# Query and key parts kept beside each other per row in DRAM: a 3 KB store per row, loads of one part of eight rows in 1 KB packets

## The reference, cut to what matters

```python
x = x + xattn0(layernorm(x), ctx, ctx)         # 16 heads of 8, softmax over 128 keys
x = x + ffn0(layernorm(x))                     # one of 8 experts per token
x = x + xattn1(layernorm(x), ctx, ctx)         # the same with a causal mask
x = x + ffn1(layernorm(x))                     # two of 8 experts per token, SiLU gate
# inside an attention: score = einsum('bhqd,bhkd->bhqk', q, k) / sqrt(8)
```

## Time and profile before

| | |
|---|---|
| time, median of 3 runs | 794.02 us (790.98 to 795.57) |
| the profiled execution | 793.19 us, its span 791.5 us |
| TensorE busy | 619.9 us (78%) |
| VectorE, ScalarE, GpSimd busy | 483.2, 392.2, 359.4 us |
| DMA | 65087 packets, 87.58 MB |
| stages in the span | projection to about 113 us, attention 0 to 261, one-expert stage to 380, attention 1 to 607, two-expert stage to 771, the end to 791 |

### The profile page before, as it was taken

One profiled execution on the slowest core, in us unless ns is written; L12 is line 12 of the kernel. 1 busy time (PEld: TensorE's weight loads), 2 busy tenths in 40 slices (PEclk: granted clock), 3 DMA queues, 4 the chain that ended last, 5 costly groups with the idle time before them and its releaser, 6 DMA issues.

```text
span 791.5 us, 22885 instructions
## 1 busy us (share of the span) xinstructions
PE 619.9 (78%) x8205; PEld 473.8 (60%) x8205; DVE 483.2 (61%) x1255; ACT 392.2 (50%) x901; POOL 359.4 (45%) x555
## 2 busy tenths in 40 slices
PE   1583548999999599999899888888740999999970
PEld 1352236777776354554566666666530999999970
DVE  1462257777773367667667988889534455555535
ACT  0684335777777224443367666666630444444430
POOL 5384351111010234445245577877874455555650
PEclk9697677999999699999799999999955999999995
DMA  3479850434400593577711543400011222222219
GB/s 75 123 249 177 189 193 3 109 95 111 96 4 2 108 268 143 188 277 247 295 49 40 102 106 106 103 26 26 26 44 54 55 66 70 59 63 67 63 34 318
DMA packets 65087, 87.58 MB, mean 111 GB/s; under 512 B 11209, under 2 KB 52433, under 8 KB 64977
## 3 DMA queue, kind: packets, MB, share of 16 engines
q1 hardware_dynamic: 56400, 75.04, 33.9%
q0 software_dynamic: 4352, 8.99, 3.6%
q10 hardware_dynamic: 4224, 2.10, 0.9%
HBM read 43.99 MB, written 41.96 MB: 109 GB/s over the span
## 4 chain that ended last, share of the span: by engine, by line
PE 36%; DVE 13%; issue 6%; POOL 5%; ACT 5%; DMA 2%; SPq 1%; ACTq 0%; POOLq 0%; DVEq 0%
PE bank L1567 12%; PE bank L1575 6%; PE bank L1410 5%; DVE nm L929 3%; POOL sorted_in L1130 2%; ACT pr L814 2%; POOL pr L1100 1%; DMA kk<-results 1%; DVE e0ch L1351 1%; PE bank L697 1%; PE bank L1555 1%; PE bank L753 1%; PE bank L1391 1%; PE bank L726 1%; PE bank L715 1%
## 5 line engine op out<-in xcount | busy, mean ns | idle before, releaser
L814 ACT ACTIVATE pr<-bank 128x512 f32<-128x512 f32 x256 | 146.9, 603 | 76.0 <-PE bank L700 73.4
L929 DVE TENSOR_REDUCE nm<-bank 128x8 f32<-128x1024 f32 x128 | 155.7, 1221 | 38.9 <-PE bank L674 37.7
L1567 PE MATMUL bank<-exxt,qq 128*128 128x128 f32 (+1 forms) x864 | 109.2, 277 | 0.7 <-ACT exxt L1605 0.7
L1567 PEld LDWEIGHTS bank<-exxt,qq 128*128 128x128 f32 (+1 forms) x864 | 101.3, 185 | 1.1 <-ACT exxt L1605 1.1
L1100 POOL TENSOR_SCALAR_AFFINE_SELECT pr<-pr 128x1024 f32<-128x1024 f32 x64 | 69.7, 1090 | 56.8 <-ACT pr L814 56.1
L1541 POOL DMA_INDIRECT results<-exy,exre x72 | 71.3, 990 | 29.8 <-issue 29.0
L715 PE MATMUL bank<-pr,values 128*9 128x128 f32 x2048 | 81.6, 278 | 2.4 <-POOL pr L1100 2.4
L697 PE MATMUL bank<-qq,kk 48*128 48x128 bf16 x1024 | 75.4, 221 | 3.4 <-ACT pr L814 2.4
L1410 PE MATMUL bank<-e0ch,expert_w 128*128 128x512 f32 x128 | 70.8, 635 | 6.4 <-DVE e0ch L1351 6.4
L700 PE MATMUL bank<-mt,pick 64*128 64x128 bf16 x1024 | 75.5, 221 | 0.0
L1642 DVE TENSOR_TENSOR exhi<-bank,exsi 128x384 f32<-128x384 f32 x72 | 40.1, 557 | 54.7 <-PE bank L1567 43.6
(11 more groups left out here) (209 smaller groups left out, 1160.9 us busy)
## 6 DMA issues: line engine op xcount, KB each, us to landing
sorted_in<-values SPq DMA_DIRECT2D x25, 715.0 KB, 5.7
k_parts<-pj_parts SPq DMA_DIRECT2D x16, 384.0 KB, 4.3
kk<-k_parts SPq DMA_DIRECT2D x64, 96.0 KB
qq<-q_parts SPq DMA_DIRECT2D x64, 96.0 KB
exx<-sorted_in SPq DMA_DIRECT2D x72, 65.0 KB
kk<-k_parts SPq DMA_DIRECT2D x64, 64.0 KB
qq<-q_parts SPq DMA_DIRECT2D x64, 64.0 KB
q_parts<-pj_parts SPq DMA_DIRECT2D x8, 384.0 KB, 4.1
```

The costliest lines, as they stand in the source:

```text
L814: act.activation(probs[c], st_bank[(n * NC + c) % ST][:], ACT.Exp, scale=scale).then_inc(exp_s, 1)
L929: dve.tensor_reduce(neg_max[n % 2][:, u * 2 * C4:(u + 1) * 2 * C4], score_banks(n, u).rearrange("q (h k) -> q h k", k=T), AX_X, ALU.max, n ...
L1567: mm = pe.matmul(to[q.p][0:fn, f * T:(f + 1) * T], own_w[q.p][:, w0 + f0:w0 + f0 + fn], x, start=True, stop=True)
```

## The change

The DRAM tensors get the part as the last index but one, so that the three parts of one row (of one head) lie beside each other, 3 KB in one piece. The store becomes one piece of 3 KB per row. One part of a head's row is now followed by the other two, so a load can take only one part of eight rows with the eight heads of a half, and each row is read in eight pieces of 1 KB that lie 3 KB apart, into 8 KB in one piece in the tile. A part that three slots need is a load for each slot, as before; the number of loads stays 12 per side.

```diff
-QK_IN = 16 * 2 * 2 * 2 * len(RUNS)
+QK_IN = 16 * 2 * 2 * 6

-        q_parts = scratch("q_parts", (NG, 3, DH, H, GT), BF16)
-        k_parts = scratch("k_parts", (2, NG, 3, DH, H, GT), BF16)
+        q_parts = scratch("q_parts", (NG, DH, H, 3, GT), BF16)
+        k_parts = scratch("k_parts", (2, NG, DH, H, 3, GT), BF16)

             for slot, part, count in runs:
-                by_half = src[part:part + count].rearrange("c d (a i) t -> a (c d) i t", a=2)
-                for s in range(2):
-                    row = s * HALF + slot * DH
-                    for u in range(2):
-                        heads = slice(u * C4, (u + 1) * C4)
-                        eng.dma_start(tile[g % QK_BUFS][row:row + count * DH, heads], by_half[s][:, heads]).then_inc(signal, 16)
+                for c in range(count):
+                    by_half = src[:, :, part + c, :].rearrange("d (a i) t -> a d i t", a=2)
+                    for half in range(2):
+                        row = half * HALF + (slot + c) * DH
+                        eng.dma_start(tile[g % QK_BUFS][row:row + DH], by_half[half]).then_inc(signal, 16)

-            eng.dma_start(to.rearrange("c d h t -> (d h) c t"), tile[:]).then_inc(signal, 16)
+            eng.dma_start(to.rearrange("d h c t -> (d h) (c t)"), tile[:].rearrange("p c t -> p (c t)")).then_inc(signal, 16)
```

## The result

The changed kernel takes 814.12 us (median of 4 runs, 808.23 to 817.54) where the kernel before takes 793.87 beside it (790.98 to 795.57): 1.0256 times the time before, 95% interval 1.0208 to 1.0304. It is slower by some 20 us. Its profiled execution took 817.03 us with a span of 815.3, against 793.19 and 791.5 before, so the two spans differ by 23.8 us, 3.6 more than the medians do.

What follows compares the result with a forecast made beforehand. The projection's second half was taken as bound by transfers, attention 0 by TensorE. Profiled 793.2 us, plus 16 for the projection and 7.5 for attention 0, gave 816.7, say 817 us; eight in ten: 794 to 866.

Steps and rivals of the forecast that it cites:

- the likeliest case: Whole kernel: a group's 24 loads take 17 to 24.6 us, total 804 to 866 us; chance 0.50.
- Eight engines a load, and the issue time not the limit: Part loads: each runs over 8 engines, 192 completions a group instead of 288; SP's 9.6 us of issue stays the faster.
- T = 19.0: Part loads, both stages: a group's 24 loads take 19.0 us instead of 12.7, bounded by 8.8 and 30.7.
- the queued row at equal crowding: Part loads: same bytes at the queued packet cost of before, 48 x 0.39 = 18.7 us a group.
- (a): Part loads: crowding becomes complete, a group takes 25 to 31 us; about 917 us at 28.9; chance 0.12.
- (b): Part loads: nothing seen, a group takes up to 13.5 us, SP's issue stays the pace; 793 +- 4; chance 0.14.
- (d): Part loads: in between, 14 to 17 us a group; projection +4 to +11, attention 0 nothing; 797 to 804; chance 0.14.
- Projection, +17 for loads and -1 for stores: Projection: three bound turns each lose 5.7 us to slower loads, less 1 for cheaper stores, +16 us.
- The gain of 0.4 us a turn: Projection stores: 3 KB packets take 2.9 instead of 3.3 us a turn, 1.2 us over three turns.
- Attention 0, +7.5 us as waits for tiles at the first scores of groups 4 to 7: Attention 0: five groups of 19.0 us loads outrun 16.7 us compute periods; group 7 arrives at 234.6, needed at 227.1.
- One-expert stage and attention 1, 0 to 3 us: Later stages: key loads grow from 15.2 to some 28 us but are covered; cost 0, at most 3 us.
- Rival (c): Projection: fewer store packets end SP's full-queue hold-ups, 5.8 us, plus 1.2 of cheaper stores; 786 us; chance 0.10.

Runs made afterwards that it cites:

- the fourth experiment: Kernel before, with loads of one eight-row part (8 KB a row) only for groups 0 to 2 in the projection; 810.43 us, 1.0218.
- the second experiment: Kernel before with only the store changed, to 3 KB pieces, its loads kept (attention values wrong, timing valid); 791.34 us, 0.9996.
- the third experiment: Kernel before, layout and store kept, every load taking one part of eight rows, 8 KB in one piece per row; 818.57 us, 1.0324.
- 5.: Kernel before, with loads of one eight-row part only for groups 3 to 7 in attention 0; 805.01 us, 1.0129.
- 6.: Kernel before, with only the key loads of groups 3 to 7 in attention 0 taking one eight-row part; 802.48 us, 1.0118.
- experiment 11: Kernel before, with all eight heads of a half in one load, six loads a side instead of 12; 802.46 us, 1.0127.
- experiment 12: Kernel before, its loads reordered so that neighbours in the queue write different halves of the rows; 786.28 us, 0.9917.
- 7.: Changed kernel, with the late loads of both attentions issued in four lots of six per group; 811.49 us, 1.0254 to the kernel before.

## Why the prediction was right, and where only by luck

817.0 us was forecast, in 804 to 866 for the likeliest case and 794 to 866 in all; 814.12 was measured. Step by step:

- **Eight engines a load, and the issue time not the limit**: right. The completions fell by 4 a load.
- **T = 19.0**: 17.7 measured in attention 0 (17.2 from first packet to last), and 0.10 us a packet, the value at which the forecast said that the sum would hold. In the projection it is not one value: 19.7, 15.8 and 14.3 us where before it is 13.1, 14.4 and 13.5. The bounds were 8.8 and 30.7, so taking the queued row at equal crowding (48 x 0.39) was the good choice. (By the port rule of the Trainium skill, page SBUF — State Buffer, section "Door 1: The DMA port swizzle", T would have been 28.9 us, an estimate load by load; the trace disagrees with it. That loads in flight on different rows overlap is my reading.) Rivals (a) and (b) fall with it, and (d), whose T of 14 to 17 is near that of the projection, falls by the time: 797 to 804 was its range.
- **Projection, +17 for loads and -1 for stores**: +11.35 measured. By the sum's own form T = 17.7 gives 3 x 5.0 x 0.9 - 1 = +12.5. But the two terms were each too small: narrow loads alone cost 20.3 us there (the fourth experiment, with 8 KB pieces), and 9 us of it come back with the layout of the change (20.3 - 11.35; single profiles, whose start of attention 0 scatters by 4 us). The gain of 0.4 us a turn counted the stores' packets; what a store also does is to hold SP when the queues are full. Freeing that was worth nothing behind the loads of before (the second experiment). That it is what gives back the 9 us behind narrow loads fits the 23.9 and 8.6 us of the third experiment, but isn't shown: the 1 KB pieces of the loads changed with it.
- **Attention 0, +7.5 us as waits for tiles at the first scores of groups 4 to 7**: this step failed. By its own form T = 17.7 leaves 1 us. 11.3 was measured, and not one wait of TensorE for `kk` or `qq`: group 3's first scores come at 171.68, on time for a stage that starts 11.35 us later. In its place stand stalls of the instruction stream, 8.0 us, with the half clock behind them, 3.3. That narrow loads in this stage bring them on is shown (5., 6.: some 10 us each, with the gaps; the fourth experiment, which has the narrow loads in the projection alone, has none), how they do is not. Narrow loads aren't needed for one either: the six long loads a side of experiment 11 have a stall of 2.1 us. The share of cost that went to the wrong mechanism was near the right size by luck: with T known, the sum would have been 13.5 us over before, and 23.8 was seen.
- **One-expert stage and attention 1, 0 to 3 us**: +0.1 together. Right, though the 36 key loads took 18.5 us (283.07 to 301.60), not 28.
- **Rival (c), the store pays by freeing SP**: seen as a mechanism (a store's issue 4.64 to 0.45 us), worth nothing by itself. It isn't only a count of packets: in experiment 12 the hold-up goes with the 1 KB pieces kept.

Open: why it is the seventh and the fifteenth of the 16 KB packets that come late in every kernel with narrow loads in attention 0 (the seventh in the changed kernel and in 3., 5., 6., the fifteenth in the changed kernel, 5. and 7.), while others come on time in the same traffic. The third experiment, with narrow loads in attention 1 as well, has the forty-first of the program late there like the changed kernel (12.0 us after the fortieth, with a stall of 1.1; 6.3 to 7.4 in the kernels without such loads there, and 7.0 when they are spread out). In the kernels with narrow loads, every gap over 10 us within the two attentions where the kernel before has less lies at the ninth, seventeenth, thirty-third or forty-first packet of the program, so on places eight apart. Smaller ones lie elsewhere: the sixteenth of the stage comes 8.3 and 9.0 us after the fifteenth, with a stall of 1.7 and 2.2 us in the changed kernel and in experiment 6. A test that wasn't made would put unread narrow loads under the ninth or the seventeenth.

## What to carry to other kernels

Read the number of completions of a load beside its rows: it tells how many engines carry it, and a stage can be bound by transfers while the mean share of the engines falls (0.89 to 0.70 here). Spread what is in flight over rows, by loads of many rows and by the order of neighbours in the queue; that was worth 0.83% here for exchanging two loops, where 1 KB pieces for 4 KB ones and a 3 KB store moved nothing by themselves. And when loads are made slower "under cover" of compute, look in the trace for the instruction packets among them, not only for the waits on tiles.

## What the runs showed of the hardware that was not expected

- An instruction stream can stall a busy engine beside slow loads: gaps of 9.4 to 15.4 us between 16 KB packets, where 4 to 8 are usual, and stops of TensorE of 1.1 to 6.5 us. After some of them the matmuls of L673 took 0.61 instead of 0.40 us, at half the clock. The runs of these kernels lie far apart, 9.3 us in the changed kernel and 11.8 in the fifth experiment (1.6 in experiment 12), but so do those with the 48 unread loads, 9.0, whose profile has no stall.
- Into eight rows, loads in pieces of 8 KB moved at 85 GB/s in the third experiment and at 71 in the fifth, those in pieces of 1 KB at 86.5; loads of 24, 16 and 8 rows reach 124, and the same in turn over halves 164.
- The same number of bytes in half as many loads made the kernel slower (1.0127).
